# Recurrent block with routed experts on one core: the input's addition to an expert tile's output moves from DVE to POOL, ahead of a gather

## The reference

```python
def _L0_ffn_ref(x, scale, centroids, up_w, down_w):
    skip = x
    xn = _rms_norm(x, scale)
    ids = jnp.argmin(_dist2(xn, centroids), axis=-1)
    out = jnp.zeros_like(x)
    for e in range(N_EXPERTS):
        h = jnp.einsum('bsd,dh->bsh', xn, up_w[e])
        a, g = jnp.split(h, 2, axis=-1)
        y = jnp.einsum('bsh,hd->bsd', a * jax.nn.silu(g), down_w[e])
        out = jnp.where((ids == e)[..., None], y, out)
    return out + skip
...
xn = _layernorm(x, axis=-1)
s = _L0_attn_ref(xn, ...)
g = _silu(_L0_ffn_ref(xn, ...))
x = x + s * g
```

## Time and profile before

| what | before |
|---|---|
| time, median of 3 runs | 433.37 us (433.2 to 434.53) |
| the profiled execution's own time | 434.73 us |
| its span in the trace | 432.9 us |
| granted PE clock, mean | 0.962 of full speed |
| busy, share of the span | PE 91%, DVE 76%, POOL 54%, ACT 53% |
| expert stage, first to last `gather_a` in the loop | 240.10 to 411.46 us |

### The profile page before, as it was taken

The page is one execution under the profiler, slowest core; times in us unless marked ns, Lnnn a source line. Parts: engine busy times, 40 slices in busy tenths (PEclk is TensorE's granted clock), DMA queues, the critical chain, the costliest instruction groups (busy, mean ns, idle before and its releaser), DMA issues.

```text
span 432.9 us, 10732 instructions
## 1 busy us (share of the span) xinstructions
PE 392.1 (91%) x2785; PEld 326.4 (75%) x2786; DVE 327.5 (76%) x829; ACT 227.3 (53%) x606; POOL 231.6 (54%) x332
## 2 busy tenths in 40 slices
PE   5489999999996999999919999999999999999992
PEld 5367777777885788888807888888888888888882
DVE  5997888877657988174895887777888777878873
ACT  1466777777871021254573555555555555655551
POOL 7246777767761022027153556666665666666541
PEclk9879999999998999999977999999999999999995
DMA  6445433554444960004110222223322223331100
GB/s 184 154 152 193 137 123 95 149 179 133 145 130 168 413 239 26 27 24 119 47 39 18 63 91 61 63 76 83 103 74 83 80 77 92 100 92 56 37 15 0
DMA packets 31517, 44.81 MB, mean 103 GB/s; under 512 B 3913, under 2 KB 25586, under 8 KB 31364
## 3 DMA queue, kind: packets, MB, share of 16 engines
q1 hardware_dynamic: 24912, 29.38, 20.6%
q0 software_dynamic: 6240, 14.71, 11.6%
q10 hardware_dynamic: 340, 0.42, 0.4%
HBM read 36.28 MB, written 15.61 MB: 120 GB/s over the span
## 4 chain that ended last, share of the span: by engine, by line
PE 55%; DMA 13%; DVE 10%; issue 7%; ACT 6%; POOL 5%; POOLq 1%; SPq 1%; ACTq 0%; DVEq 0%
PE bank L558 16%; PE bank L576 11%; PE bank L397 7%; PE bank L446 6%; DMA xs<-in_x 6%; DMA row_a<-rows_a,slot_id 6%; PE bank L541 3%; PE bank L478 3%; PE bank L530 2%; ACT d_hi L734 2%; PE bank L450 2%; ACT up_hi L696 2%; POOL inv_std L1147 1%; DVE d_lo L1081 1%; POOL rs L1166 1%
## 5 line engine op out<-in xcount | busy, mean ns | idle before, releaser
L1081 DVE TENSOR_TENSOR d_lo<-down_sb,d_hi 128x1024 fp32r<-128x1024 f32 x39 | 47.8, 1225 | 31.9 <-ACT d_hi L734 31.9
L1209 POOL DMA_INDIRECT row_a<-rows_a,slot_id x39 | 40.2, 1030 | 52.3 <-DVE e_o L1095 50.3
L734 ACT ACTIVATE d_hi<-down_sb 128x1024 fp32r x39 | 41.4, 1061 | 44.5 <-PE bank L576 32.0
L1241 POOL DMA_INDIRECT out_x<-e_o,slot_id x39 | 44.7, 1147 | 21.5 <-issue 14.4
L558 PE MATMUL bank<-up_hi,e_xh 128*128 x156 | 52.8, 420 | 0.0
L1215 POOL DMA_INDIRECT row_s<-rows_s,slot_id x39 | 41.4, 1062 | 15.7 <-issue 11.6
L558 PE MATMUL bank<-up_lo,e_xh 128*128 x156 | 49.1, 396 | 0.0
L558 PE MATMUL bank<-up_hi,e_xl 128*128 x156 | 48.9, 395 | 0.0
L664 ACT ACTIVATE junk<-bank 128x256 bf16<-128x256 f32 x96 | 36.1, 380 | 23.0 <-PE bank L401 22.5
L397 PE MATMUL bank<-w_hi,x_hi 128*128 128x264 f32 (+1 forms) x128 | 42.8, 416 | 3.3 <-DVE k_sp L881 2.9
L687 ACT ACTIVATE junk<-bank 128x256 bf16<-128x256 f32 x32 | 11.9, 381 | 61.5 <-PE bank L480 57.1
(11 more groups left out here) (210 smaller groups left out, 1036.2 us busy)
## 6 DMA issues: line engine op xcount, KB each, us to landing
up_raw<-in_up_w SPq DMA_DIRECT2D x8, 1024.0 KB, 13.7
rows_a<-xn SPq DMA_DIRECT2D x32, 128.5 KB, 2.4
xs<-in_x SPq DMA_DIRECT2D x8, 512.0 KB, 3.4
down_sb<-in_down_w SPq DMA_DIRECT2D x8, 512.0 KB, 4.2
rows_a<-in_x SPq DMA_DIRECT2D x8, 512.0 KB, 4.9
rows_s<-s_out SPq DMA_DIRECT2D x8, 256.0 KB, 2.3
blk_tab<-in_blocks SPq DMA_DIRECT2D x1, 1024.0 KB, 6.6
row_a<-rows_a,slot_id POOLq DMA_INDIRECT x39, 3.4
```

The lines of the kernel that those rows point to most:

```text
L734: act.activation(d_hi[:, :, :], down_sb[:, bass.ds(e, 1), :, :].rearrange("p a c n -> p (a c) n"), ACT.Copy).then_inc(d_high, 1)
L1081: V.tensor_tensor(d_lo[:, :, :], down_sb[:, bass.ds(e, 1), :, :].rearrange("p a c n -> p (a c) n"), d_hi[:, :, :].bitcast(F32), ALU.subtra ...
L1209: G.indirect_dma_start(row_a[s % 4][:, :], None, rows_a, bass.IndirectOffsetOnAxis(ap=slot_id[:, s:s + 1], axis=0), bounds_check=N - 1, oo ...
L1241: G.indirect_dma_start(out, bass.IndirectOffsetOnAxis(ap=slot_id[:, s:s + 1], axis=0), e_o[s % 4][:, :], None, bounds_check=N - 1, oob_is_ ...
```

## The change

The sum L1095 is taken out of DVE's step and made by POOL (`add_input`), in the same loop, ahead of the gather that takes the buffer over. POOL waits for the product of that slot (`sg_done`), adds, signals `o_done`, and then waits for its own `o_done` before it issues the gather. The last four slots have the addition ahead of their scatter.

```diff
@@ DVE, step_c
                     V.tensor_tensor(o[:, :], e_z[b][:, :], row_s[(k - 2) % 4][:, :], ALU.mult).then_inc(sg_done, 1)
-                    dve.wait_ge(sg_done, s - 1)
-                    V.tensor_tensor(o[:, :], o[:, :], row_a[(k - 2) % 4][:, D + 1:2 * D + 1], ALU.add).then_inc(o_done, 1)
@@ POOL
             def gather_a(s):
 
-                after(pool, o_done, s - 3)
+                if s >= 4:
+                    pool.wait_ge(o_done, s - 3)
                 G.indirect_dma_start(row_a[s % 4][:, :], None, rows_a,
...
+            def add_input(s):
+
+                pool.wait_ge(sg_done, s + 1)
+                G.tensor_tensor(e_o[s % 4][:, :], e_o[s % 4][:, :], row_a[s % 4][:, D + 1:2 * D + 1],
+                                ALU.add).then_inc(o_done, 1)
+
...
             for s in range(4, ST):
+                add_input(s - 4)
                 gather_a(s)
                 gather_s(s)
                 scatter(s - 4)
             for s in range(ST - 4, ST):
+                add_input(s)
                 scatter(s)
```

## The result

| | before | after |
|---|---|---|
| median of the runs | 433.77 us (4 runs, 433.2 to 434.53) | 449.76 us (4 runs, 447.89 to 456.27) |
| ratio, 95% interval | | 1.0353 (1.0308 to 1.0398) |
| profiled execution, span | 432.9 us | 448.8 us |
| first to last `gather_a` in the loop | 171.36 us, 5.04 a slot | 188.48 us, 5.54 a slot |

The forecast was 461.6 us with a range from 440 to 466. The sign and the mechanism are there; the size is 15 us by the ratio and 16 by the medians, in place of 28.

What follows compares the result with a forecast made beforehand. The two-slot gather loop, 5.045 us a slot, was taken to set the pace, PE's own work just under it. Held slots 28.0 us, last slot 0.46, less 0.3: 433.37 + 28.2 = 461.6 us, range 440 to 466.

Steps and rivals of the forecast that it cites:

- The loop: Turn to product to gather to turn two steps on, 10.09 us; each us added between product and gather costs 17.5 us.
- Nothing for what DVE saves: The 39 sums of 0.42 us leaving DVE gain nothing, since `d_lo` waits for ACT's `d_hi`.
- The second piece: From the product's end to the gather's start: 1.24 us before, 1.70 by the longer path alone.
- the held state: Each late `gather_s` starts within `d_lo` and delays the next gather; self-sustaining, with no exit seen, 5.845 us a slot.
- the first piece: From PE's turn to the end of DVE's product, 5.45 us, taken as unchanged.
- The hold: A POOL DMA instruction that begins while `d_lo` runs is held until it ends and finishes about 0.88 us later.
- T: Time of one slot, taken as one value for all: 5.845 us with `gather_s` held, 5.045 before.
- 0.46 on top: Once more at the last slot, whose last scatter stands behind the last sum: 0.46 us longer.
- B: Rival: some slots held, others not, for instance through slow transfers; 446 to 454 us, chance 0.05.
- A: Rival: longer path alone, `gather_s` not held or the holding ends by itself; +8.5 us, 441.9 us, chance 0.17.
- C: Rival: not slower, the gather following POOL's addition by 0.31 us, not 0.78; 430.4 or 433 us, chance 0.06.
- POOL full or nearly: POOL's list of work takes 5.21 us a slot, just under 5.275, so any stretched DMA instruction becomes path.

Runs made afterwards that it cites:

- E4: Kernel before with the addition on neither engine, gather and scatter waiting for the product: 428.22 us, ratio 0.9835.
- E9: Kernel before with no addition on either engine and one small POOL operation, waited for, in the gather's path: 430.63 us, ratio 0.9916.
- E1: Changed kernel with `d_lo` reading its second input from PSUM in place of `d_hi`: 439.72 us, ratio 1.0093.
- E2: Kernel before, addition still on DVE, with one small POOL operation, waited for, ahead of the gather: four runs from 441.27 to 451.83 us.
- E5: Kernel before with two POOL clears of 256 numbers behind each scatter, reading nothing: 435.02 us, ratio 1.0002.
- E3: Kernel before, with an extra POOL addition of 256 numbers behind each scatter, for which no gather waits: 448.6 us, ratio 1.0284.
- E10: Changed kernel run once more, unchanged, for a second trace: 453.17 us, ratio 1.0453.
- E11: Changed kernel run a third time, unchanged, for a third trace: 449.39 us, ratio 1.0362.
- E8: Changed kernel with DVE's product moved ahead of `e_hl` and PE taking the `d_lo` group before the `e_hl` group: 455.05 us, ratio 1.047.

## Why the prediction was right in kind, and 12 us too high

**Where the gather stands.** It is on the path because it starts 3.40 us ahead of its turn, two thirds of a step (310.99 and 314.39 in the earlier trace rows); the description of the kernel, which has it about two steps ahead, is wrong there.

**The loop, and 17.5 us for each us of distance: right.** E4 and E9 have the gather 0.78 and 1.06 us behind the product, the kernel before 1.24, and the times follow, until PE's own work takes over at 4.86.

**Nothing for what DVE saves: right.** `d_lo` waited 29.1 us for ACT's `d_hi` in 35 steps, as before, and E9 leaves nothing for DVE's time to explain.

**The second piece, 1.70 taken, 1.50 measured.** The addition took 0.65 and not the 0.74 of POOL's other operation, the release 0.09 and not 0.18; the 0.78 to the gather was right. In the held state the piece was to be 2.84 and is 2.73, a slot 5.845 and is 5.745. The 0.11 of the piece makes 0.055 of this 0.10; most of the rest is the first piece, 5.45, read at a step that is one of four: in the long held stretch every fourth step takes 5.46 from turn to product's end, the others 5.37. Over 35 slots this is 0.10 x 35 = 3.5 us of the error.

**The hold: right in cause and price.** It was to end `gather_s` 0.88 behind `d_lo`; 0.87 at the first one. E1 takes it away by the operand alone. E2 enters it without the addition on POOL, E5 loads POOL without entering it. What the Trainium skill says of such an instruction, that it doesn't stall the making of descriptors (page "SBUF — State Buffer", section "Who interferes with whom", with a reason marked there as inferred), doesn't hold for these indirect DMAs: 1.96 us in place of 1.00. The other sentence of that section, on two SBUF inputs against a reading GpSimd instruction, agrees with E1 and E3.

**The step that failed: "the held state feeds itself and I see nothing that leaves it".** It feeds itself, but 15 of 35 `gather_s` were not stretched. I had put one T for all slots. The loop is two steps long, so there are two of them, one for even slots and one for odd, and what the loop fixes is only the sum of two periods. The kernel before shows this already: its gathers are apart by a longer and a shorter period in turn, 5.23 and 4.85 us around the one at 310.99 in the earlier trace rows, and those rows give the distance behind the product for one of the two alone:

```profile
305.76 1.02 POOL L1209 DMA_INDIRECT row_a<-rows_a,slot_id  x1 [1.18 <-DVE e_o L1095]
...
315.84 1.03 POOL L1209 DMA_INDIRECT row_a<-rows_a,slot_id  x1 [1.19 <-DVE e_o L1095]
```

In the changed kernel, held, the two drift apart. In the middle of the long held stretch gathers are 5.76 and 5.67 apart (290.94, 296.70, 302.37), at its end 6.09 and 5.45:

```profile
348.21 1.03 POOL L1208 DMA_INDIRECT row_a<-rows_a,slot_id  x1 [0.78 <-POOL e_o L1240]
354.30 1.02 POOL L1208 DMA_INDIRECT row_a<-rows_a,slot_id  x1 [0.78 <-POOL e_o L1240]
359.75 1.03 POOL L1208 DMA_INDIRECT row_a<-rows_a,slot_id  x1 [0.78 <-POOL e_o L1240]
361.09 1.00 POOL L1214 DMA_INDIRECT row_s<-rows_s,slot_id  x1 [0.31 <-issue]
361.13 1.23 DVE L1081 TENSOR_TENSOR d_lo<-down_sb,d_hi 128x1024 fp32r<-128x1024 f32 x1 [0.79 <-ACT d_hi L734]
```

`d_lo` starts T - 2.15 behind the product, where T is now the gap between two turns, and `gather_s` 2.73 + 1.33 = 4.06, so a gap of 6.2 us lets `gather_s` through, where my 5.845 was safe. At 264.35 it is through by 0.15, at 361.09 by 0.04. The trace also shows where the drift comes from. From the turn of slot 12 to that of slot 24 the even slots need 69.32 us, the odd ones from 11 to 23 need 68.81. Of the 0.51 between them 0.28 lie between turn and product, where every fourth step, the first of the four that the loop over i writes out, takes the 5.46 in place of 5.37 and is an even one; 0.25 lie between the gather's start and the turn, which takes 3.19 to 3.53. So half of the drift is in the order of the program and returns in every execution, which fits the likeness of E10 and E11, and half is in the landing of the gathers. What makes that step longer wasn't looked into.

By the count of `gather_s`, 15 free slots at 5.745 - 5.156 = 0.59 are 8.9 us. With the 3.5 above that is 12.4, and 28.2 - 12.4 = 15.8 us; the span grew by 15.9. That it meets so well is partly luck. With the held `gather_a` only 13 of the loop's 34 periods are free, and the loop grew by 188.48 - 171.36 = 17.1 us. What stands behind its last gather became shorter, 448.8 - 428.70 = 20.1 us in place of 432.9 - 411.46 = 21.4, where I had put 0.46 on top. Of those 0.46, 0.44 did come, between the last product and the end of the last scatter (2.67 us in place of 2.23); but the last gathered rows are turned 2.15 us behind their gather's start, where it was 3.18, and the last steps are shorter too.

**Rivals.** B, held in part, was the outcome, its bracket 446 to 454; I had given it 0.05, as I looked for a cause of release in slow transfers only. A, the path alone, is what E1 measures: 4.3 us over before in place of 8.5, since the piece is 1.50. The slow landings that I named under B make about half of the drift. C asked for 0.31 between addition and gather; it is 0.78 in every slot.

**POOL full or nearly.** I had its list at 5.21 against a loop of 5.275. It is 0.02 + 0.65 + 0.78 + 1.03 + 0.31 + 1.00 + 0.30 + 1.03 = 5.12. In the free stretch, with 5.156 a slot, list and loop (10.35 / 2 = 5.175 by 5.45 + 1.50 + 3.40) can't be told apart; E8 shows that the list alone is a bound.

## What to carry to other kernels

An operation moved from a busy engine to one with idle time is not free if it lands in front of something for which a third engine waits: read the distance from the last input to the transfer's start, and divide by the number of steps over which the loop closes. Look next at what a shift of some tenths of a us lets coincide: here a DMA instruction that in every second slot had started 0.13 us ahead of a long DVE instruction fell behind its start, and that cost nearly three times what the shift itself did. And where a loop closes over two steps, work out both phases, since an average of the two can call a state stable that one of them leaves.

## What the runs showed that I had not expected

- The hold is mutual: around a POOL addition of 0.67 us DVE's product took 0.65 us in place of 0.42 and its sum 0.72 (E3). Two clears of 256 numbers on POOL, about 0.58 us, ran over the sum and left it at 0.42 to 0.43 (E5).
- Reading the second operand from PSUM left `d_lo` at 1.22 us and freed POOL from it (E1).
- POOL's sum of 128x256 float32 takes 0.646 us, its product of the same shape 0.738.
- An operation of 0.20 us on POOL cost 5.9 us in the lowest run and 10.8 in the profiled one, as it stood in the gather's path in all 35 slots (E2).
